# A fused attention and feed-forward kernel: another order of the opening, and no constant products on TensorE

## The reference, cut to what matters

```
def layer(x):                                   # x: [2, 1024, 512]
    x = x + LN(attention(LN(x)))                # LN: (x - mean) / sqrt(var + 1e-5)
    x = x + LN(ffn(LN(x)))
def attention(x):                               # 16 query heads, 4 key/value heads, 128 wide
    q, k, v = x @ Wq.T, x @ Wk.T, x @ Wv.T
    q, k = rope(q), rope(k)                     # q*cos + rotate_half(q)*sin
    qf, kf = elu(q) + 1, elu(k) + 1             # = min(exp, 1) + relu
    state_s = sum over s' <= s of kf_s' v_s'^T ; z_s = sum over s' <= s of kf_s'
    return (qf_s state_s / (qf_s z_s + 1e-6)) @ Wo.T
def ffn(x):                                     # 2048 hidden
    h = silu(x @ Wg) * (x @ Wu)
    keep the 2 of each 4 neighbours of h that are largest in magnitude
    return h @ Wd
```

## Time and profile before

| | |
|---|---|
| median of 3 runs | 1243.27 us (1241.34 to 1243.37) |
| profiled execution | 1244.04 us, of which its span is 1242.2 us |
| PE busy | 1207.5 us, 97% of the span |
| DVE, ACT, POOL busy | 737.5, 549.0, 507.8 us |
| mean granted TensorE clock | 0.988 |

### The profile page before, as it was taken

The page is one execution under the profiler, slowest core; times in us unless marked ns, Lnnn a source line. Parts: engine busy times, 40 slices in busy tenths (PEclk is TensorE's granted clock), DMA queues, the critical chain, the costliest instruction groups (busy, mean ns, idle before and its releaser), DMA issues.

```text
span 1242.2 us, 16141 instructions
## 1 busy us (share of the span) xinstructions
PE 1207.5 (97%) x6047; PEld 1016.9 (82%) x6047; DVE 737.5 (59%) x1220; ACT 549.0 (44%) x1058; POOL 507.8 (41%) x458
## 2 busy tenths in 40 slices
PE   8699999999999999999998999999999999999996
PEld 7588888888888888888887878888888878888884
DVE  7465656554756465647554365667556755555577
ACT  3365554555555546555555433333323333323322
POOL 5332533332546324334245534342425643333314
PEclk9799999999999999999999999999999999999997
DMA  5412231222343313222223312121113321211103
GB/s 191 111 43 68 78 78 42 77 52 52 89 114 102 94 38 82 69 71 76 51 68 109 117 65 71 45 73 34 52 51 102 111 77 43 60 43 60 35 1 118
DMA packets 50349, 90.31 MB, mean 73 GB/s; under 512 B 6496, under 2 KB 6752, under 8 KB 50272
## 3 DMA queue, kind: packets, MB, share of 16 engines
q1 hardware_dynamic: 50272, 89.29, 25.3%
HBM read 64.09 MB, written 8.39 MB: 58 GB/s over the span
## 4 chain that ended last, share of the span: by engine, by line
PE 85%; DVE 7%; ACT 2%; issue 2%; DMA 1%; POOL 1%; SPq 1%; DVEq 0%; ACTq 0%
PE bank_q L454 8%; PE bank_q L452 8%; PE bank_q L453 8%; PE bank_od L452 4%; PE bank_od L453 4%; PE bank_od L454 4%; PE bank_t L452 4%; PE bank_t L454 4%; PE bank_t L453 4%; PE bank_y L454 4%; PE bank_y L452 4%; PE bank_y L453 4%; PE bank_od L558 4%; PE bank_od L561 3%; PE bank_s L452 3%; PE bank_s L453 3%
## 5 line engine op out<-in xcount | busy, mean ns | idle before, releaser
L1140 POOL TENSOR_TENSOR w_lo<-stage,w_hi 128x512 fp32r<-128x512 f32 x96 | 129.3, 1361 | 252.2 <-ACT w_hi L711 251.0
L452 PE MATMUL bank_q<-x_hi,w_hi 128*128 128x512 f32 x440 | 176.9, 402 | 0.0
L454 PE MATMUL bank_q<-x_lo,w_hi 128*128 128x512 f32 x440 | 172.7, 393 | 0.0
L453 PE MATMUL bank_q<-x_hi,w_lo 128*128 128x512 f32 x440 | 172.2, 391 | 0.0
L1140 POOL TENSOR_TENSOR big_lo<-hidden,big_hi 128x512 fp32r<-128x512 f32 x32 | 73.5, 2319 | 214.4 <-ACT big_hi L831 214.4
L822 ACT ACTIVATE scratch<-hidden 128x512 f32<-128x512 f32 x64 | 40.6, 634 | 206.9 <-DVE hidden L1063 206.9
L1140 POOL TENSOR_TENSOR big_lo<-q_rows,big_hi 128x1024 fp32r<-128x1024 f32 x32 | 78.6, 2456 | 90.4 <-ACT big_hi L753 90.4
L965 DVE TENSOR_SCALAR small<-bank_od 128x4 f32<-128x4 f32 x61 | 9.6, 157 | 161.0 <-PE bank_od L561 101.3
L1079 DVE TENSOR_TENSOR y_acc<-bank_od,y_acc 128x512 f32<-128x512 f32 x44 | 30.2, 686 | 118.9 <-PE bank_od L454 118.9
L454 PE MATMUL bank_y<-wout_lo,a_hi 128*128 128x512 f32 x256 | 99.9, 390 | 0.0
L452 PE MATMUL bank_y<-wout_hi,a_hi 128*128 128x512 f32 x256 | 99.9, 390 | 0.0
(11 more groups left out here) (230 smaller groups left out, 3063.4 us busy)
## 6 DMA issues: line engine op xcount, KB each, us to landing
q_rows<-scratch SPq DMA_DIRECT2D x124, 128.0 KB, 2.3
x_rows<-x SPq DMA_DIRECT2D x56, 256.0 KB, 3.0
stage<-wq SPq DMA_DIRECT2D x32, 256.0 KB, 2.7
stage<-wo SPq DMA_DIRECT2D x32, 256.0 KB, 2.6
stage<-wg SPq DMA_DIRECT2D x32, 256.0 KB, 2.7
stage<-wu SPq DMA_DIRECT2D x32, 256.0 KB, 2.7
stage<-wd SPq DMA_DIRECT2D x32, 256.0 KB, 2.7
x<-x_rows SPq DMA_DIRECT2D x16, 256.0 KB, 2.5
```

The source lines that it names most:

```text
L452: pe.matmul(ps, whi, xhi, start=first, stop=False, skip_group_check=True)
L453: pe.matmul(ps, wlo, xhi, start=False, stop=False, skip_group_check=True)
L454: return pe.matmul(ps, whi, xlo, start=False, stop=last, skip_group_check=True)
L1140: return pool.tensor_tensor(dst, full, hi.bitcast(F32), ALU.subtract)
```

## The change

1. PE loses all 47 `warm` products and the tile of ones.
2. PE's opening becomes: turn tiles 0-3; queries 0, 1, 2; turn tiles 4-7; queries 3; keys 0; values 0; queries 4, 5; keys 1; turn_values 0; turn_keys 0. The first query projection takes its four products with `x_lo` last and waits for `x_lo` only there. `keys(1)` leaves slot 0.
3. Tile 7 has bank_t to itself. `values(0)`, the turned values and the turned keys of the opening have banks of their own (bank_y, bank_st, bank_y) in place of bank_t.
4. The weight plan begins with the four query pieces, then key and value. SP's order of loads follows; the cosine and sine tables come later, and the rotated pairs 0, 1 and 2 are all moved in the opening (pair 2 was in slot 0). DVE rotates pair 2 in the opening too.
5. Tiles 4 to 7 are normalised by POOL's `scaling` and ACT, no longer by DVE.
6. Epsilon is added on DVE, in all 64 normalisations, in an instruction behind the variance; POOL only takes the power.
7. The low parts of pieces 6 and 7 go from DVE to POOL. The orders on ACT, DVE and POOL in the opening are new.

```diff
-SCALED = LATER + ENDING
+SCALED = FIRST[4:] + LATER + ENDING
 def weight_plan():
-    plan = [(("k", 0, 0), -1), (("q", 0, 0), -1), (("q", 0, 1), -1), (("q", 0, 2), -1), (("v", 0, 0), -1),
-            (("q", 0, 3), -1)] + [(("o", 0, h), -1) for h in range(4)]
+    plan = [(("q", 0, i), -1) for i in range(4)] + [(("k", 0, 0), -1), (("v", 0, 0), -1)]
+    plan += [(("o", 0, h), -1) for h in range(4)]
 def by_dve(piece):
-    return piece[0] == "o" and piece[1] == 0 and piece[2] < 2 or piece[0] == "d" and piece[2] == 3
+    return piece[0] == "d" and piece[2] == 3
 def turn_bank(k):
-                return [psS, psO, psD, psY, psS, psY, psSt, psS][k]
+                return [psS, psO, psD, psY, psS, psY, psSt, psT][k]
 # SP
+            load_piece(3)
             tables(0)
-            for t in range(4, TT):
-                rows_in(t)
-            for k in range(3, 6):
-                load_piece(k)
-            tables(1)
+            load_piece(4)
+            load_piece(5)
             sp.dma_start(mask[:, :], causal).then_inc(mask_ld, 16)
             for k in range(6, 10):
                 load_piece(k)
             pair_rows(0)
-            pair_rows(1)
+            tables(1)
             for k in range(10, OPEN):
                 load_piece(k)
+            pair_rows(1)
+            for k in range(OPEN, OPEN + 2):
+                load_piece(k)
+            pair_rows(2)
 # PE
+            def project_first(ps, i, half):
+                cuts = [slice(kk * P, (kk + 1) * P) for kk in range(KT)]
+                for kk, c in enumerate(cuts):
+                    pe.matmul(ps, Wh[i][:, c], Xh[:, half, kk, :], ...)
+                    pe.matmul(ps, Wl[i][:, c], Xh[:, half, kk, :], ...)
+                g.wait_ge(dve_xl, 4)
+                for kk, c in enumerate(cuts):
+                    ins = pe.matmul(ps, Wh[i][:, c], Xl[:, half, kk, :], ...)
+                return ins
 def keys(p):
-                g.wait_ge(act_ktr, p)
+                if p == 1:
+                    g.wait_ge(dve_k1, 1)
+                else:
+                    g.wait_ge(act_ktr, p)
-            warm(24)
             g.wait_ge(ident_ld, 16)
-            for job, count in zip(FIRST[:4], (3, 0, 8, 12)):
+            for job in FIRST[:4]:
                 turn(job)
-                warm(count)
-            keys(0)
-            for i in range(4):
-                queries(i)
+            split_wait(g, ("q", 0, 0))
+            g.wait_ge(act_xh, 4)
+            project_first(psQ[:, 0, :], 0, 0).then_inc(pe_q, 1)
+            queries(1)
+            queries(2)
             for job in FIRST[4:]:
                 turn(job)
+            turned[0] = TT
+            queries(3)
+            keys(0)
             values(0)
             queries(4)
+            queries(5)
+            keys(1)
             turn_values(0)
-            queries(5)
             turn_keys(0)
 # ACT, the new opening in full
+            split_x(FIRST[0]); split(0); split_x(FIRST[1]); split_x(FIRST[2]); split(1)
+            split_x(FIRST[3]); split(2); split(3)
+            normalise(FIRST[4]); normalise(FIRST[5]); split(4); split(5)
+            normalise(FIRST[6]); normalise(FIRST[7]); split(6); split(7)
+            split_x(FIRST[4]); split_x(FIRST[5]); split(8)
+            split_x(FIRST[6]); split_x(FIRST[7]); split(9)
+            query_terms(0); swap_keys(0); query_split(0); key_terms(0); query_terms(1)
+            key_split(0); take_values(0); query_split(1); values_split(0); turned_split(0)
 # DVE
-                dve.bn_aggr(mv[q % 4], stat[q % 4]).then_inc(dve_var, 1)
+                dve.bn_aggr(mv[q % 4], stat[q % 4]).then_inc(dve_agg, 1)
+                g.wait_ge(dve_agg, q + 1)
+                dve.tensor_scalar(mv[q % 4][:, 1:2], mv[q % 4][:, 1:2], EPS_LN, None, ALU.add).then_inc(dve_var, 1)
+            variance(0); variance(1); normalise(0); variance(2); variance(3)
+            normalise(1..3); split_x(0..3); variance(4..7)
+            rotate(0); rotate_sum(0); split_x(4..7); rotate(1); rotate_sum(1)
+            query_sum(0); rotate_keys(0); key_sum(0); query_sum(1); rotate(2); rotate_sum(2)
 # POOL
-                pool.tensor_tensor(rstd[q % 4], mv[q % 4][:, 1:2], eps_ln, ALU.add).then_inc(pool_eps, 1)
-                g.wait_ge(pool_eps, q + 1)
-                pool.tensor_tensor(rstd[q % 4], rstd[q % 4], mhalf, ALU.pow).then_inc(pool_rs, 1)
+                pool.tensor_tensor(rstd[q % 4], mv[q % 4][:, 1:2], mhalf, ALU.pow).then_inc(pool_rs, 1)
+            deviation(0..3); split(0); split(1); wait dve_nm >= 4
+            scaling(4); scaling(5); split(2); scaling(6); scaling(7); split(3..9)
+            query_low(0); key_low(0); query_low(1); split(10); split(11)
```

More of the change, by code:

```diff
@@ L207, in build @@
         Wl = [w_lo[:, i, :] for i in range(6)] + [Kl[:, :], Ul[:, :]]
-        mhalf, eps_den, eps_ln, sign = [small[:, i:i + 1] for i in range(4)]
+        mhalf, sign = small[:, 0:1], small[:, 3:4]
         Dh = [D0h[:, :], Ah[:, :, :].rearrange("p c d -> p (c d)"), D2h[:, 0:W]]
@@ L256, in build, with value_bank, turned_values_bank, turned_keys_bank @@
         psX = [psY, psSt]
+        def value_bank(p):
+            return psT if p else psY
+        def turned_values_bank(p):
+            return psT if p else psSt
+        def turned_keys_bank(p):
+            return psT if p else psY
         def down_bank(y):
@@ L427, in _ @@
             pair_rows(0)
-            pair_rows(1)
+            tables(1)
             for k in range(10, OPEN):
                 load_piece(k)
-            for k in range(OPEN, RING_W + OPEN):
+            pair_rows(1)
+            for k in range(OPEN, OPEN + 2):
+                load_piece(k)
+            pair_rows(2)
+            for k in range(OPEN + 2, RING_W + OPEN):
                 load_piece(k)
@@ L434, in _ @@
                 tick = tick_a(i) if kind == "a" else tick_f(i)
-                if kind == "a" and i % 2 == 0 and i <= 58:
+                if kind == "a" and i % 2 == 0 and 0 < i <= 58:
                     pair_rows((i + 4) // 2)
@@ L491, in values @@
                 split_wait(g, ("v", p // 2, 0))
[L492 to L493 removed]
+                if p:
+                    g.wait_ge(dve_k1, p + 1)
+                project(value_bank(p)[:, :], 5, p // 8 * 2 + p % 2).then_inc(pe_v, 1)
             turned = [0]
@@ L599, in slot_a @@
                 p = s // 4 + 1
-                if 1 <= p < STEPS and s == k_slot(p):
+                if 2 <= p < STEPS and s == k_slot(p):
                     keys(p)
@@ L846, in _ @@
             split(3)
-            swap_keys(0)
+            for job in FIRST[4:6]:
+                normalise(job)
             split(4)
             split(5)
+            for job in FIRST[6:]:
+                normalise(job)
+            split(6)
+            split(7)
+            split_x(FIRST[4])
+            split_x(FIRST[5])
+            split(8)
+            split_x(FIRST[6])
+            split_x(FIRST[7])
+            split(9)
+            query_terms(0)
+            swap_keys(0)
+            query_split(0)
             key_terms(0)
-            split(6)
+            query_terms(1)
             key_split(0)
[L853 to L857, removed]
             take_values(0)
-            query_split(0)
+            query_split(1)
             values_split(0)
-            query_terms(1)
             turned_split(0)
-            query_split(1)
             for k in range(10, OPEN):
@@ L960, in slot_a @@
                 before = at(tick - 1, lambda j: turn_tick(*j), [j for j in TURNS if j in LATER])
-                if s % 2 == 0 and s + 4 < 2 * STEPS * 2:
+                if s % 2 == 0 and 0 < s and s + 4 < 2 * STEPS * 2:
                     rotate((s + 4) // 2)
@@ L1102, in _ @@
             variance(FIRST[2])
-            normalise(FIRST[1])
             variance(FIRST[3])
-            normalise(FIRST[2])
-            split_x(FIRST[0])
-            normalise(FIRST[3])
             for job in FIRST[1:4]:
+                normalise(job)
+            for job in FIRST[:4]:
                 split_x(job)
[L1110 to L1117, removed]
+            for job in FIRST[4:]:
+                variance(job)
+            rotate(0)
+            rotate_sum(0)
+            for job in FIRST[4:]:
+                split_x(job)
+            rotate(1)
+            rotate_sum(1)
+            query_sum(0)
             rotate_keys(0)
             key_sum(0)
[L1120 to L1127, removed]
             query_sum(1)
+            rotate(2)
+            rotate_sum(2)
             for kind, i in TICKS:
@@ L1214, in _ @@
                 deviation(job)
-            g.wait_ge(dve_nm, 4)
             split(0)
             split(1)
-            deviation(FIRST[4])
-            deviation(FIRST[5])
+            g.wait_ge(dve_nm, 4)
+            for job in FIRST[4:6]:
+                scaling(job)
             split(2)
[L1221 to L1225, removed]
+            for job in FIRST[6:]:
+                scaling(job)
```

(6 more changed lines are left out.)

41 lines of the change are left out of this document (18 added, 23 removed).

## The result

The changed kernel takes 1232.55 us (median of 4, 1232.11 to 1234.01) against 1242.3 (4 runs): ratio 0.9927, 95% interval 0.9913 to 0.9942, so 9 to 10 us or 0.7% faster. Forecast were 1231.2 and 12 us of gain. The time lies in the range and the direction was right; a fifth to a quarter of the gain is missing. The profiled execution took 1234.01 us, the longest of the four, with a span of 1232.1.

What follows compares the result with a forecast made beforehand. PE was taken as the bound, with slot 2 starting 12.6 us earlier: span 1242.2 - 12.6 + 0.5 (clock) = 1230.1, time 1231.9, predicted 1231.2 as the profiled run lay 0.8 above the median; range 1226.0 to 1236.5.

Steps and rivals of the forecast that it cites:

- the 0.5 for the clock: First quotients' turn: a possible clock fall after a 2.5 us wait, 1.6 to 2.4 us lost, counted as a third.
- epsilon: All 64 normalisations: DVE gains a 0.2 us addition each, showing only at the end; -0.4 to +0.5 us, taken as 0.
- The scores: Opening, slot 0: scores at 43.6 us (42.7 to 45.5), after a PE wait of 1.2 us instead of 4.2.
- 0.75 us by the row: rotate_sum on DVE beside POOL's low part: 1.967 us against 1.215, up to 0.75 each, put in for pairs 0 and 2.
- The wait at k0: Opening, after q3: rotate(1) at 27.8 just as q3 is done; no PE idle over 0.5 us between 13 and 42.
- the ring: Opening: loads 7 and 8 wait for pieces 3 and 4 to be split, delaying x_hi; x_lo of tile 7 ready at 27.6.
- The clock at the start: First dense products from 12.8 us: 4.5 us at the low clock, 2.1 us lost.
- rival A: Opening: the clock rises late, after 10.6 us, costing 2.9 us more, time 1234.0; chance 0.12.
- The clock at the scores: Slot 0 scores: the pause of 1.2 us is too short, so no slow stretch was counted.
- a third of a loss: First quotients' turn: clock fall after the 2.5 us wait uncertain, so 0.5 us counted of 1.6 to 2.4.
- Rival E: Better than summed: a short landing (2.3) and no clock drop at 661 us, time 1227; chance 0.05.
- One off the end for each microsecond: Slot 2 onward: every microsecond by which slot 2 starts earlier comes off the end, unless something new stalls behind it.

Runs made afterwards that it cites:

- the repetition: The changed kernel run again unchanged, on one chip beside the other experiments: 1233.4 us, ratio 0.9933 to the kernel before.
- constants back: The 47 constant (warm) products put back where they stood, against the changed kernel: 1236.5 us, ratio 0.9958 to the kernel before.
- both together: Changed kernel with pair 0 issued ahead of load 9, its accompanying ACT and split moves, and epsilon back on POOL: 1229.34 us, ratio 0.9907 to the kernel before.
- epsilon on POOL: Changed kernel with epsilon added on POOL again for all normalisations: 1230.59 us, ratio 0.9908 to the kernel before.
- earlier pair 0: Changed kernel with pair 0 issued ahead of load 9, x_hi of tiles 4 to 7 ahead of piece 7's cast, piece 9 split later: 1233.21 us.
- key's low part first: Changed kernel with POOL's key_low(0) ahead of query_low(0): 1235.12 us, ratio 0.9947 to the kernel before.
- epsilon on POOL at the end: Changed kernel with epsilon back on POOL for the last eight tiles only: 1232.83 us, ratio 0.9928 to the kernel before.
- The kernel before at one look: The kernel before, unchanged, run once more to see when the clock rises with the constant products in place: 1241.44 us.

## Why the prediction was right, and what was mis-sized

Right in order, place and nearly in time (here the profile of the changed kernel): tile 0's turn (6.3 foretold, 6.26), the first projection (12.8; 13.41 here, 12.78 in the repetition), rotate(1) (27.8; 27.86), scores (43.6; 45.06), quotients' turn (54.0; 54.80), slot 2 (57.2; 58.03). The mechanism was as told: PE is the bound, the wait for tile 7 goes, the wait at the scores halves, a new one comes at the quotients (1.5 us, foretold 2.5).

From the profile before to the profile after, 12.6 us of lead at slot 2 were foretold less 0.5 for the clock, 12.1 in the span. Measured were 11.8 at slot 2, 11.5 at the first silu, 10.5 at the last and 10.1 in the span: 0.8 are missing in the opening, 0.3 up to the feed-forward part, 1.0 in it and 0.4 in the tail, and the 0.5 for the clock was not needed.

- **The term that was mis-sized is epsilon.** The prediction said: "It shows only at the end, where DVE is the last link; bounds -0.4 to +0.5 us, taken as 0." Moving it back gives 2.8 us. It had the size of one addition right (0.2 us) and the place, and did not multiply by the eight tiles that follow each other on DVE there: 8 x 0.22 = 1.8 us, measured 1.7. The other 1.0 us came in the middle, where DVE was counted as having "500 idle" us. Why PE feels an addition there, that it stands between instructions that free PE's banks, is argued from the order and not tested. In the profile from which the forecast started, the low clock in the tail hid all but 0.4 us of the tail's part. That was luck: without it the miss would have been 1.3 us larger, though still in the range.
- **The scores.** The chain was 1.5 us longer than foretold (45.06 - 43.6). 1.6 us of it is the DVE instruction behind POOL's low part (2.28 in place of 0.69), for which ACT's key_terms(0) and then query_terms(1) waited; with it short, the sum of pair 1 started 1.6 us earlier (38.58 in place of 40.18). The prediction had weighed this for pair sums, at 0.75 us by the row, and not for the key's sum. For pair 2's sum, which it had put in, 2.23 us were measured against 1.23 alone, so 1.0 us, between the row's 0.75 and the 1.2 that it worked out by the Trainium skill. The Trainium skill (SBUF — State Buffer, Who interferes with whom) says that a DVE instruction with two SBUF inputs contends with a GpSimd instruction that reads SBUF, and that the shared port pair is an exclusive lock. This trace agrees: DVE's sum ended 0.55 us after POOL's instruction.
- **The wait at k0.** Foretold as none; 1.74 us, since the chain through the ring (load 7, then `x_hi`, `x_lo` of tile 7) ended at 27.95 as computed (27.6), but PE was ready at 26.35, 1.4 us early, thanks to the clock. In the repetition, with the clock up 5 us later, there was no such wait.
- **The clock at the start.** Taken as 4.5 us at the low level, 2.1 us lost. Measured 0 in the profile of the changed kernel and 3.2 to 5.7 us in the eight others without constants: the estimate was fair, and rival A (10.6 us) did not occur. The Trainium skill (TensorE: Matmul & The Clock Gate, Why this matters for your kernels) advises to run products first, there so that a benchmark is accurate. This case agrees in part: in three of the four profiles with constants the clock was up sooner. But it is worth less here than the constants cost: putting them back lost 3.1 us.
- **The clock at the scores.** "With so short a pause I count no slow stretch" was said of 1.2 us, and the pause was twice that. Pauses there of 2.23 (changed kernel), 2.64 (constants back) and 2.48 us (both together) left the clock up, those of 2.43 (repetition), 2.27 (epsilon on POOL), 2.48 (earlier pair 0) and 4.11 us (key's low part first) were followed by 3.4 us at the low level, 1.6 us lost, and one of 2.66 us (epsilon on POOL at the end) by 6.8. At the quotients' turn, where a third of a loss was counted, the clock fell in none of these profiles, not even after 2.63 us (constants back). Rival E's other part, no fall near 661 us, came true in half: the fall near 655 us is there in four of the nine profiles with the new opening (the changed kernel's among them) and missing in five (the repetition's among them).
- **"One off the end for each microsecond".** Not quite. The kernel before at one look against the repetition of the changed one, from their traces: 11.1 us apart at the first quotients' turn, 10.6 at the tenth, 10.0 at the 21st, 11.3 at the 41st, 9.8 at the 57th, 11.3 at the last and at the first silu, 10.3 at the last silu, 8.7 at the end. The step from 9.8 to 11.3 is the fall of the clock at 661 us (3.4 us), which only the kernel before had here. So the lead moves up and down in the attention slots and has lost 1.3 us by the 57th turn, for which no cause was looked for; it loses 1.0 and 1.6 us behind them, where epsilon's additions lie.

What stays open: whether the moves of pair 0 gain anything beside epsilon; what moves the lead by 1.3 us in the attention slots; and what makes the clock rise at 13 us in one execution and at 18 in another of the same kernel.

## What to carry to other kernels

A small instruction that is moved to an engine with 40% idle time costs nothing only where that engine is not the last link: count how often it stands in a back-to-back chain (here the last tiles), and multiply. Read a whole tile's period on each engine near the end, since the bound there is often another engine than in the rest. Filler products for the clock are paid for in the path ahead of the first real product; compare when that one starts, not only how fast it runs. And ask whether PE waits anyway before the next link of the chain: here a clock that came 5 us later moved the scores by 0.1 us.

## What the runs showed of the hardware

- A DVE instruction with two SBUF inputs, 0.69 us alone, took 2.28 us when POOL's 2.41 us instruction had started 0.68 us before it, and ended 0.55 us behind that.
- The granted clock in the profile reads 1.00 until the first rise, though products of 128 x 512 took 0.43 us then (repetition of the changed kernel), as with PEclk 0.50 later.
- PE busy for 13.5 of 14 us with 128-column products and transposes did not bring the full clock before 18.8 us in one execution (constants back); in another, of the changed kernel, it was up between 12.6 and 13.4 us, after 16 transposes and ahead of any projection product.
- Pauses of PE of 2.2 to 2.7 us at the same place left the clock up in three executions and were followed by 3.4 or 6.8 us at the low level in four.
